# GELU experts: finished tiles scattered to token order as they are made, both picks loaded back plainly

## The reference

```python
def _moe_forward(x, gate_w, gate_b, fc1_w, fc1_b, fc2_w, fc2_b, alpha):    # 8 experts, K = 2
    xf = x.reshape(-1, H_)
    top_val, top_idx = jax.lax.top_k(xf @ gate_w + gate_b, K)
    gate_score = jax.nn.softmax(top_val, axis=-1)
    onehot = jax.nn.one_hot(top_idx, E, dtype=xf.dtype)
    comb = jnp.einsum('tk,tke->et', gate_score, onehot) * alpha[:, None]
    # for each expert e, added up:
    #   y = gelu(xf @ fc1_w[e] + fc1_b[e]) @ fc2_w[e] + fc2_b[e];  out += y * comb[e][:, None]
x = x + 0.5 * _L1_ffn_ref(_layernorm(x, axis=-1), ...)      # stage 3
x = x + _L1_attn_ref(_layernorm(x, axis=-1), ...)           # stage 4, the delta net
x = x + 0.5 * _L1_ffn_ref(_layernorm(x, axis=-1), ...)      # stage 5, the last one
```

## Time and profile before

| | us |
|---|---|
| median of three runs | 2441.1 |
| the profiled execution, its own time | 2445.81 |
| its span, first to last instruction | 2444.1 |
| stage 3, layer norm to last sum | 439 to 703.6 |
| stage 5, layer norm to last sum | 2171 to 2436.8 |
| TensorE busy | 2069.8 (85%) |
| VectorE busy | 1286.1 (53%) |
| ScalarE busy | 999.1 (41%) |
| GpSimd busy | 391.8 (16%) |
| mean granted TensorE clock | 0.921 |

### The profile page before, as it was taken

How to read it: one execution, slowest core, us unless ns; L and a number is a source line. 1 busy time by engine, 2 the same in 40 slices (tenths; PEclk the granted TensorE clock), 3 DMA queues, 4 the chain that set the end, 5 groups by cost and what they waited for, 6 DMA issues and landing times. The chain is left out here.

```text
span 2444.1 us, 52330 instructions
## 1 busy us (share of the span) xinstructions
PE 2069.8 (85%) x20606; PEld 1507.8 (62%) x20606; DVE 1286.1 (53%) x2928; ACT 999.1 (41%) x2476; POOL 391.8 (16%) x442
## 2 busy tenths in 40 slices
PE   7889989598824698999999999999999998958884
PEld 4543355487722467677767766776677666737774
DVE  4434444412225466776677667766776775531222
ACT  2113321222202355646664655565556654512221
POOL 0001100110020022122212222122122211202002
PEclk9969989699956699999999999999999998958997
DMA  1100001721011110111011101110111010045001
GB/s 45 34 11 1 1 14 39 278 76 27 16 44 42 22 31 14 34 26 31 19 35 24 32 19 36 23 32 19 36 24 32 19 28 10 11 137 205 30 20 61
DMA packets 148345, 100.08 MB, mean 41 GB/s; under 512 B 88640, under 2 KB 134992, under 8 KB 148112
## 3 DMA queue, kind: packets, MB, share of 16 engines
q1 hardware_dynamic: 144368, 86.59, 12.5%
q0 software_dynamic: 3744, 10.23, 1.5%
HBM read 83.28 MB, written 13.50 MB: 40 GB/s over the span
## 5 line engine op out<-in xcount | busy, mean ns | idle before, releaser
L1582 PE MATMUL dn_ps<-xnT,dn_w 128*128 128x512 f32 x512 | 260.3, 634 | 33.6 <-DMA dn_w<-in_W_qkvz_dram 22.1
L1935 DVE SCALAR_TENSOR_TENSOR dn_cv<-dn_raw,dn_cw,dn_cv 128x1024 f32<-128x1024 f32 x192 | 270.6, 1409 | 1.2
L588 PE MATMUL g_ps<-g_w,xnT 128*128 (+1 forms) x736 | 166.1, 379 | 0.0
L1582 PEld LDWEIGHTS dn_ps<-xnT,dn_w 128*128 128x128 f32 x512 | 91.5, 198 | 114.9 <-issue 100.2
L577 PE MATMUL g_ps<-g_xT,g_w_now 128*128 128x128 f32 x960 | 117.5, 282 | 50.3 <-DVE g_w_now L716 50.3
L1727 PE MATMUL dn_ps<-dn_wout,dn_oT 128*128 128x256 f32 x512 | 150.0, 418 | 6.2 <-ACT dn_oT L1742 3.7
L1742 ACT ACTIVATE dn_kdk<-dn_ps,dn_cf 128x128 f32<-128x128 f32 x256 | 80.0, 364 | 180.4 <-PE dn_ps L1622 180.4
L516 ACT ACTIVATE xnT<-g_ps,g_b_now 128x128 f32<-128x128 f32 x240 | 68.4, 368 | 206.3 <-PE g_ps L577 206.3
L577 PEld LDWEIGHTS g_ps<-g_xT,g_w_now 128*128 128x128 f32 x960 | 112.6, 196 | 61.5 <-issue 61.5
L588 PEld LDWEIGHTS g_ps<-g_w,xnT 128*128 128x128 f32 x736 | 136.4, 190 | 16.7
L1742 ACT ACTIVATE dn_raw<-dn_ps 128x512 f32<-128x512 f32 x128 | 76.4, 598 | 147.1 <-PE dn_ps L1582 147.1
(11 more groups left out here) (309 smaller groups left out, 4375.8 us busy)
## 6 DMA issues: line engine op xcount, KB each, us to landing
g_w<-in_fc_dram SPq DMA_DIRECT2D x32, 1024.0 KB, 13.0
dn_w<-in_W_qkvz_dram SPq DMA_DIRECT2D x16, 768.0 KB, 4.5
dn_x<-dn_cum_rows SPq DMA_DIRECT2D x32, 256.0 KB, 3.9
ys_rows<-g_ys SPq DMA_DIRECT2D x46, 128.0 KB, 1.7
dn_wout<-in_W_out_dram SPq DMA_DIRECT2D x16, 256.0 KB, 2.8
f_gate<-in_gateT_dram SPq DMA_DIRECT2D x16, 128.0 KB, 2.2
f_up<-in_upT_dram SPq DMA_DIRECT2D x16, 128.0 KB, 2.3
f_down<-in_downT_dram SPq DMA_DIRECT2D x16, 128.0 KB, 2.4
```

The lines of the kernel that those rows point to most:

```text
L588: last = pe.matmul(y_b[i % 2][:, 0:D], hT[i % 2][:, f, :], of(f), start=(f == 0), stop=(f == NF - 1))
L1582: mm = pe.matmul(to, w[:, k, W_COL[u] * P:(W_COL[u] + 1) * P], m.xnT[:, k, b * T:(b + 1) * T], start=(k == 0), stop=(k == KD - 1))
L1935: ins = nc.vector.scalar_tensor_tensor(out=cv[:, u], in0=raw[:, u, :, tap:tap + T], scalar=cw[:, g, tap:tap + 1], in1=cv[:, u], op0=ALU.mu ...
```

## The change

Each finished tile is no longer stored in tile order and fetched back by index. It is scattered: one indexed DMA on GpSimd's queue writes each of its 128 rows to row `token + 1024 * pick` of `ys_rows`. All empty slots write row 2048, which nobody reads. After the last tile SP's queue loads both picks with 16 plain DMAs of 128 consecutive rows each.

For that, routing has to know by slot whether the pick is a first or a second one: `token` gets a third plane (`R_BACK`), the matmul L545 becomes 69 columns wide instead of 46, and `place_u` is now made by slot, after `token_u`. VectorE's four bias adds move ahead of all sums.

```diff
@@ constants: R_BACK = R_TILE + 2 * NT, 16 more columns; SPARE = 2 * NTOK; ys_rows has SPARE + P rows @@
+    back = (SPARE - NTOK * (np.arange(2 * NT) // NT)).astype(np.float32)
@@ SP @@
-            for i in range(TILES):
-                sp.wait_ge(y_copied, i + 1)
-                sp.dma_start(tile_rows(ys_rows, i), ys[:, i % 3, :]).then_inc(ys_stored[i % 3], 16)
+            sp.wait_ge(y_copied, TILES)
             for n in range(3):
                 sp.wait_ge(ys_stored[n], 16 * ((TILES - n + 2) // 3))
+            for t in range(NT):
+                for r in range(2):
+                    sp.dma_start(gathered[r][:, t, :], tile_rows(ys_rows, r * NT + t)).then_inc(ys_back[t], 16)
@@ GpSimd @@
-            for i in range(TILES):
+            def fetch(i):
                 if i >= RING:
                     pool.wait_ge(turned, i - RING + 1)
                 nc.gpsimd.indirect_dma_start(xs[:, i % RING, :], None, xn_rows, ...)
+            def put_back(i):
+                pool.wait_ge(y_copied, i + 1)
+                if i >= 1:
+                    pool.wait_ge(ys_stored[(i - 1) % 3], 16 * ((i + 2) // 3))
+                nc.gpsimd.indirect_dma_start(ys_rows, bass.IndirectOffsetOnAxis(ap=place_u[:, i:i + 1], axis=0),
+                                             ys[:, i % 3, :], None).then_inc(ys_stored[i % 3], 16)
+            for i in range(RING):
+                fetch(i)
             pool.wait_ge(place_ready, 1)
-            for n in range(3):
-                pool.wait_ge(ys_stored[n], 16 * ((TILES - n + 2) // 3))
-            for t in range(NT):
-                for r in range(2):
-                    j = r * NT + t
-                    nc.gpsimd.indirect_dma_start(gathered[r][:, t, :], None, ys_rows, ...)
+            for i in range(TILES):
+                if i + RING < TILES:
+                    fetch(i + RING)
+                put_back(i)
@@ TensorE @@
-                last = pe.matmul(y_b[0][:, 0:2 * TILES], in_slot[:, j, :], token[:, j]..., 
+                last = pe.matmul(y_b[0][:, 0:3 * TILES], in_slot[:, j, :], token[:, j]...,
@@ VectorE @@
+            nc.vector.tensor_tensor(token[:, :, 2, :], in_tile[:], over_tiles(route[:, R_BACK:R_BACK + 2 * NT]), ALU.mult)...
-            chain(nc.vector.scalar_tensor_tensor(out=place_f[:], in0=tile_f[:], scalar=float(P), in1=slot[:], ...))
-            nc.vector.tensor_copy(place_u[:], place_f[:]).then_inc(place_ready, 1)
+            (after owner) chain(nc.vector.scalar_tensor_tensor(out=place_f[:], in0=in_tile[:, 0, :], scalar=float(SPARE), ...))
+            nc.vector.tensor_tensor(place_u[:], place_f[:], in_tile[:, 2, :], ALU.subtract).then_inc(place_ready, 1)
+            for g in range(4):
+                dve.wait_ge(b2_ready, g + 1)
+                two = m.x[:, 2 * g:2 * g + 2, :].rearrange("p t d -> p (t d)")
+                nc.vector.tensor_tensor(two, two, h_b[g], ALU.add).then_inc(b2_added, 1)
             for t in range(NT):
-                if t % 2 == 0:
-                    (the same wait and add, for t // 2)
```

More of the change, by code:

```diff
@@ L335 @@
 TILES = E1 + NTOK * 2 // P - 1
-SLOTS = TILES * P
 RING = 6
@@ L342 @@
 R_PART, R_TILE = R_SLOT + P, R_SLOT + P + 1
-R_WIDTH = R_TILE + 2 * NT
+R_BACK = R_TILE + 2 * NT
+R_WIDTH = R_BACK + 2 * NT
+SPARE = 2 * NTOK
 def route_constants():
@@ L359, in route_constants @@
     tile = np.tile(P * np.arange(NT), 2).astype(np.float32)
+    back = (SPARE - NTOK * (np.arange(2 * NT) // NT)).astype(np.float32)
     spread = lambda a: np.broadcast_to(a, (P, len(a)))
     part = r[:, None].astype(np.float32)
-    return np.ascontiguousarray(np.concatenate([before, ones, groups, count, spread(rows), part, spread(tile)], axis=1))
+    return np.ascontiguousarray(np.concatenate([before, ones, groups, count, spread(rows), part, spread(tile), spread(back)], axis=1))
 def moe_gelu(nc, m, tag, gate, gate_bias, fc1, fc1_b, fc2, fc2_b, alpha, iota_in, route_in, xn_rows, ys_rows):
@@ L392, in moe_gelu @@
         held = sb("held", [P, 2 * NT, E1])
-        rank_f, tier, slot, held_first, tile_f, place_f = (sb(n, [P, 2 * NT]) for n in (
-            "rank_f", "tier", "slot", "held_first", "tile_f", "place_f"))
+        rank_f, tier, slot, held_first, tile_f = (sb(n, [P, 2 * NT]) for n in (
+            "rank_f", "tier", "slot", "held_first", "tile_f"))
         above = sb("above", [P, 2 * NT, E1 - 1])
-        place_u = sb("place_u", [P, 2 * NT], U32)
+        place_f = sb("place_f", [P, TILES])
+        place_u = sb("place_u", [P, TILES], U32)
         in_slot = sb("in_slot", [P, 2 * NT, P], BF16)
         in_tile = sb("in_tile", [P, 2 * NT, TILES])
-        token = sb("token", [P, 2 * NT, 2, TILES], BF16)
+        token = sb("token", [P, 2 * NT, 3, TILES], BF16)
         token_u = sb("token_u", [P, TILES], U32)
@@ L539, in _ @@
             pe.matmul(y_b[1][:, P:P + E1], totals[:], route[:, R_GROUP + P:R_GROUP + P + E1], start=True, stop=True).then_inc(ranks_ready, 1)
-            pe.wait_ge(token_ready, 2)
+            pe.wait_ge(token_ready, 3)
             for j in range(2 * NT):
@@ L544, in _ @@
                     pe.wait_ge(in_slot_ready, j // 4 + 1)
-                last = pe.matmul(y_b[0][:, 0:2 * TILES], in_slot[:, j, :], token[:, j].rearrange("p a n -> p (a n)"),
+                last = pe.matmul(y_b[0][:, 0:3 * TILES], in_slot[:, j, :], token[:, j].rearrange("p a n -> p (a n)"),
                                  start=(j == 0), stop=(j == 2 * NT - 1))
@@ L675, in _ @@
             nc.vector.tensor_tensor(token[:, :, 1, :], in_tile[:], over_tiles(route[:, R_TILE:R_TILE + 2 * NT]), ALU.mult).then_inc(token_ready, 1)
+            nc.vector.tensor_tensor(token[:, :, 2, :], in_tile[:], over_tiles(route[:, R_BACK:R_BACK + 2 * NT]), ALU.mult).then_inc(token_ready, 1)
             for q in range(4):
@@ L679, in _ @@
                                         route[:, None, R_SLOT:R_SLOT + P].broadcast_to([P, 4, P]), ALU.is_equal).then_inc(in_slot_ready, 1)
-            chain(nc.vector.scalar_tensor_tensor(out=place_f[:], in0=tile_f[:], scalar=float(P), in1=slot[:], op0=ALU.mult, op1=ALU.add))
-            nc.vector.tensor_copy(place_u[:], place_f[:]).then_inc(place_ready, 1)
             dve.wait_ge(tokens_found, 1)
-            chain(nc.vector.tensor_copy(in_tile[:, 0:2, :], y_b[0][:, 0:2 * TILES].rearrange("p (a n) -> p a n", a=2)))
+            chain(nc.vector.tensor_copy(in_tile[:, 0:3, :], y_b[0][:, 0:3 * TILES].rearrange("p (a n) -> p a n", a=3)))
             nc.vector.tensor_tensor(token_u[:], in_tile[:, 0, :], in_tile[:, 1, :], ALU.add).then_inc(tokens_ready, 1)
@@ L689, in _ @@
             nc.vector.tensor_copy(owner[:], owner_f[:]).then_inc(owner_ready, 1)
+            chain(nc.vector.scalar_tensor_tensor(out=place_f[:], in0=in_tile[:, 0, :], scalar=float(SPARE), in1=in_tile[:, 1, :],
+                                                 op0=ALU.add, op1=ALU.add))
+            nc.vector.tensor_tensor(place_u[:], place_f[:], in_tile[:, 2, :], ALU.subtract).then_inc(place_ready, 1)
             dve.wait_ge(exp_ready, 1)
@@ L734, in _ @@
             copy_y(TILES - 1)
+            for g in range(4):
+                dve.wait_ge(b2_ready, g + 1)
+                two = m.x[:, 2 * g:2 * g + 2, :].rearrange("p t d -> p (t d)")
+                nc.vector.tensor_tensor(two, two, h_b[g], ALU.add).then_inc(b2_added, 1)
             for t in range(NT):
-                if t % 2 == 0:
-                    dve.wait_ge(b2_ready, t // 2 + 1)
-                    two = m.x[:, t:t + 2, :].rearrange("p t d -> p (t d)")
-                    nc.vector.tensor_tensor(two, two, h_b[t // 2], ALU.add).then_inc(b2_added, 1)
                 dve.wait_ge(b2_added, t // 2 + 1)
@@ L2079, in build @@
         load_inputs(nc, m, a["x"], const(a["c_table"], C_EYE))
-        xn_rows, ys_rows = (nc.dram_tensor(f"{n}_rows", (rows, D), F32).ap() for n, rows in (("xn", NTOK), ("ys", SLOTS)))
+        xn_rows, ys_rows = (nc.dram_tensor(f"{n}_rows", (rows, D), F32).ap() for n, rows in (("xn", NTOK), ("ys", SPARE + P)))
         for s in stages:
```

2 lines of the change are left out of this document (removed).

## The result

| | before | changed |
|---|---|---|
| median of 9 runs, us | 2441.36 | 2426.06 |
| lowest to highest | 2438.06 to 2452.33 | 2417.66 to 2432.67 |
| profiled execution / span | 2445.81 / 2444.1 | 2426.55 / 2424.8 |

The ratio is 0.993, 95% interval 0.9912 to 0.9948: the changed kernel is faster by 12.7 to 21.5 us of 2441.36, around 17; the two medians lie 15.3 us apart. A second set, 6 runs of the changed kernel against 11 of before, gives medians of 2421.82 and 2443.88 and a ratio of 0.991 (0.9891 to 0.9929). The forecast, 19.6 us less (a ratio of 0.992), lies in both intervals.

A forecast was written before the change was run, and what follows sets the result against it. GpSimd's issue of 16 indexed fetches, 20.2 us, was taken to bound each stage's end. Ends -20.6 us, routing +1.0, so -19.6: profiled 2445.8 to 2426.2, median 2441.1 to 2421.5; range 2417.5 to 2430.

The forecast's parts named there:

- likeliest case: Whole kernel: the change works as forecast, 2421.5 us, own range 2419 to 2424.5; chance 0.76.
- GpSimd's answer, 0.7 us: Stage end: GpSimd starts the last scatter 0.7 us after T, the last `ys` copy's end; bounds 0 and 0.9.
- should be down by then: Stage end: the scatter before the last, issued 3.5 us earlier, should have landed when the last one starts.
- The scatter, 2.8 us: Stage end: the last tile's scatter, most likely all 128 rows to row 2048, lands in 2.8 us; bounds 2.3 and 3.8.
- Rival B: Last tiles' scatters: writes to one row queue up, +8.8 us in two stages, 2430; mild B, C, D together 0.13.
- First loads at T + 3.55, first sum at T + 6.55: Stage end: SP answers the scatter's landing in 0.05 us; the bias adds end at T + 6.55 in stage 3.
- The loads keep up with VectorE: Stage end: 16 plain loads follow every 0.54 us and land in 2.3, nearly equal to VectorE's sums, 8.3 us.
- rival C: Stage end: plain loads slower than 0.54 us each; half way 2429, in full 2442; full B or C 0.03.
- The end: Both stages: last sum at T + 14.95 in place of T + 25.2 and T + 25.3, 20.6 us gained.
- Routing, +0.5 us a stage: Routing before the first token fetch: the third product and wider matmuls add 0.5 us a stage, 1.0 us in all.
- The loop, nothing: Tile loop: GpSimd's two DMAs, 2.5 us of a period of at least 7.2, and two new waits cost nothing.
- rival A: Tile loop: scatter and weight copy block each other; at 0.9 us a tile 27 us, 2448; chance 0.08.

The follow-up runs named there:

- experiments 2 and 3: Changed kernel, 16 plain loads replaced by GpSimd indexed fetches (2) or issued by GpSimd (3): last sum 27.45/27.37 and 16.64/16.94 us after the last `ys` copy.
- experiment 5: Changed kernel, but empty slots write 128 different rows, 2048 + p, in place of row 2048: last sum 14.67 and 14.70 us after the last `ys` copy.
- Experiment 6: Changed kernel, with the second picks loaded by ScalarE's queue and the first by SP: last sum 15.26 and 15.63 us after the last `ys` copy.
- Experiment 7: Changed kernel without the third plane, one index for fetch and scatter: token indices 30.52 us after the layer norm's start in both stages, against 31.07 and 31.10.
- experiment 4: Changed kernel with two extra token fetches before the scatter in each tile from 8 on: tile period 9.11 us, last sum 19.04 and 19.56 us after the last `ys` copy.

## Why the prediction was right

Its time was right, and its mechanism in the main: the ends were bound by GpSimd's issue of indexed fetches, experiments 2 and 3 show it from both sides. That the profiled execution lost 19.3 us, so near the 19.6 forecast, is in part luck: the ends gave 1.7 us less than forecast, and 1.4 us came back from the way to T, the step behind the last sum and stretches that the change doesn't touch. The median, 2426.06, lies in the range that was given, 2417.5 to 2430, but above the likeliest case's own, 2419 to 2424.5. Point by point:

- **GpSimd's answer, 0.7 us.** Measured 0.69 and 0.67, but for another reason than the one given, and that the number fits is luck. I took it as the time that GpSimd needs after a copy; that is 0.27, as the other scatters and experiment 5 show. The start came 0.75 us after the landing of scatter 21, which "should be down by then" and came within 0.1 us of T. The row that the 0.7 was read from was also misread: that store landed at 2411.48 + 1.66 = 2413.14, not at 2413.28, so GpSimd's start at 2413.97 was 0.83 after it.
- **The scatter, 2.8 us.** Measured 3.1, and 2.4 for full tiles. Rival B's mechanism is there in small: 128 writes to one row cost 0.7 us, plus 0.4 through the chained wait. It took 1.1 us a stage of the gain. That reads of one row cost 0.9 more stays an estimate: in every run the empty slots read one row.
- **First loads at T + 3.55, first sum at T + 6.55.** Measured T + 3.95 and 4.25, and T + 6.74 and 6.94: 0.3 of it is the scatter, the rest SP's answer, 0.16 and 0.47 in place of 0.05.
- **The loads keep up with VectorE.** This step failed in size. I priced the issue, 0.54 us (measured 0.475), and added a fixed landing of 2.3. With many in flight they land in 2.0 to 3.6, and VectorE waited 0.8 and 0.6 us in all between its sums: 9.05 and 8.87 us from first to last in place of 8.3. That is 0.05 us a sum, under the 0.1 that was to tell of rival C, but five single waits are 0.15 to 0.38. Experiment 6 shows that the landing depends on how many are in flight: with twice the issue rate the median grew to 4.8.
- **The end.** T + 14.95 forecast, T + 15.8 measured, 18.9 us gained in place of 20.6.
- **Routing, +0.5 us a stage.** Measured 0.55 and 0.57 up to `token_u`, and 0.6 and 0.2 at T, where other differences come in. Experiment 7 takes it back up to `token_u`.
- **The loop, nothing.** Right; the scatters beside the weight stream landed in 4.8 us at most, and the period is 9.11. Of rival A's contention there are 0.13 us, in a half that is covered, and they did not decide anything.
- **Rival C** named the right place, the loads, and overrated it.

## What to carry to other kernels

Where results must be permuted, put the indexed side of the traffic where its queue has idle time (here 2.5 us of a 9 us tile), and leave only plain transfers for the part that everything waits for: on GpSimd an indexed DMA of 128 rows took 1.26 us from issue to issue, a plain one 0.53. Padding that must be written somewhere goes to different rows; of what was tried on the changed kernel this shortened its ends most, by 1.1 us each. When a chain of waits is put between DMAs to keep them in order, look at the last two links: here a landing that took 0.7 us longer cost that and 0.4 us more, since the next DMA's start followed it and no longer VectorE's copy.

## What the runs showed of the hardware that was not expected

- GpSimd issues a plain DMA of 128 rows every 0.53 us and an indexed one every 1.26 (experiments 2 and 3).
- A scatter whose 128 rows of 1 KB all go to one row lands in 3.1 us, one to different rows in 2.4 (experiment 5).
- GpSimd's start after a wait is 0.27 us or 0.7, and the traces show which. Where a wait instruction of its own stands before the DMA (POOLq) and ends late, the DMA starts 0.70 us after that instruction's end: in the last scatter of the changed kernel (2402.48 to 2403.18), in the first fetch at the end of the kernel before (2413.28 to 2413.97) and in 27 of the extra fetches of experiment 4. Where that instruction had long passed and the late count is one that the DMA itself waits for, it is 0.27, as in 44 of the changed kernel's 46 scatters. Why the two differ is left open.
- Where the weight copy (0.69 us for 1,024 elements a lane) and GpSimd's indexed DMA overlap, one of the two takes 0.1 to 0.4 us longer, not a whole instruction.
- In stage 3 of experiments 2 and 3, where GpSimd issued the last DMAs, VectorE's first work of the next stage began 3.3 and 2.5 us after the last sum, against 1.35 in the changed kernel. That GpSimd issued last is not enough to explain it: in the kernel before it did so too, and there it was 1.6 us. The cause is open.
